# The first chunk of a convolution and mixture-of-experts kernel: another way of preparing it

## The reference, cut to what matters

```
conv: y = conv3x3(sign(ln_c(x)), sign(w) * sw)      # binarised, sw a power of two per channel
      mean, var = y over images and places, per channel
      clip((y - mean) * rsqrt(var + 1e-5) * gamma + beta, -1, 1)
ffn on tokens t (one per image and place, 64 channels), after a layernorm over channels:
      feat = mean over the 32 images               # per place
      w    = softmax(feat @ Wr + br)               # 8 experts, per place
      y    = for each expert: relu(bn(.@W1)) -> relu(bn(.@W2)) -> @Wo + bo
      sum over the experts with weights w
```

## Time and profile before

| what | us |
|---|---|
| median of 3 runs | 1387.19 (1386.34 to 1387.43) |
| the profiled execution, its own time | 1392.51 |
| its span, first to last instruction | 1390.7 |
| last convolution result copied by ACT, start | 168.69 |
| `t` of chunk 0, start | 178.27 |
| first `layer2` of chunk 0, start on PE | 218.24 |
| mean granted clock of TensorE, share of full | 0.982 |

### The profile page before, as it was taken

The page is one execution under the profiler, slowest core; times in us unless marked ns, Lnnn a source line. Parts: engine busy times, 40 slices in busy tenths (PEclk is TensorE's granted clock), DMA queues, the critical chain, the costliest instruction groups (busy, mean ns, idle before and its releaser), DMA issues. The chain is left out here.

```text
span 1390.7 us, 36592 instructions
## 1 busy us (share of the span) xinstructions
PE 1315.8 (95%) x14782; PEld 662.3 (48%) x14782; DVE 889.0 (64%) x1592; ACT 868.4 (62%) x1151; POOL 550.1 (40%) x474
## 2 busy tenths in 40 slices
PE   5899838999999999999999999999999999999997
PEld 3577613444544454445444444444454445444443
DVE  4344525676776666776667666666777666766665
ACT  4567645666666666666666666666666666666643
POOL 0514022344443444443444443444442544443441
PEclk9999958999999999999999999999999999999999
DMA  8978612232333232333232333232333223333121
GB/s 181 178 183 182 125 27 61 48 68 63 74 73 80 50 67 64 79 68 81 48 68 62 75 74 81 48 67 65 76 71 78 51 63 65 75 75 72 32 54 28
DMA packets 251009, 107.15 MB, mean 77 GB/s; under 512 B 238864, under 2 KB 239088, under 8 KB 250864
## 3 DMA queue, kind: packets, MB, share of 16 engines
q1 hardware_dynamic: 249600, 103.49, 35.4%
q0 software_dynamic: 1264, 1.61, 0.7%
HBM read 78.97 MB, written 26.09 MB: 76 GB/s over the span
## 5 line engine op out<-in xcount | busy, mean ns | idle before, releaser
L913 DVE SCALAR_TENSOR_TENSOR v<-ps,negb,wb 128x448 f32<-128x448 f32 x896 | 571.0, 678 | 298.7 <-PE ps L572 297.6
L743 ACT ACTIVATE h<-ps,bias 128x896 f32<-128x896 f32 x448 | 451.3, 1007 | 323.4 <-PE ps L550 323.4
L550 PE MATMUL ps<-xc,w 64*64 64x448 f32 x3584 | 463.0, 542 | 12.7 <-POOL xc L422 11.5
L588 PE MATMUL ps<-v,wo 64*64 64x448 f32 x3584 | 461.2, 540 | 3.9 <-issue 3.1
L572 PE MATMUL ps<-h,w 64*64 64x448 f32 x3584 | 457.3, 541 | 4.2 <-issue 1.8
L588 PEld LDWEIGHTS ps<-v,wo 64*64 64x64 f32 x3584 | 173.0, 133 | 186.5 <-issue 171.3
L550 PEld LDWEIGHTS ps<-xc,w 64*64 64x64 f32 x3584 | 163.6, 132 | 185.3 <-issue 179.9
L572 PEld LDWEIGHTS ps<-h,w 64*64 64x64 f32 x3584 | 169.4, 133 | 158.4 <-issue 141.1
L452 POOL TENSOR_TENSOR o<-o,upper 128x448 f32<-128x448 f32 x112 | 127.4, 1138 | 289.1 <-DVE o L923 289.1
L444 POOL TENSOR_TENSOR o<-xin,gconst 128x448 f32<-128x448 f32 x112 | 130.6, 1186 | 238.0 <-ACT gconst L786 144.2
L422 POOL TENSOR_TENSOR xc<-xc,spread 128x896 f32<-128x896 f32 x56 | 122.5, 2205 | 209.4 <-DMA spread<-rs_rows 209.4
(11 more groups left out here) (143 smaller groups left out, 669.0 us busy)
## 6 DMA issues: line engine op xcount, KB each, us to landing
xa<-in_x SPq DMA_DIRECT2D x64, 392.0 KB, 6.9
xin<-in_x SPq DMA_DIRECT2D x112, 224.0 KB, 4.1
spread<-rs_rows SPq DMA_DIRECT2D x112, 224.0 KB, 4.2
out<-o SPq DMA_DIRECT2D x224, 112.0 KB, 2.5
rs_rows<-rs SPq DMA_DIRECT2D x112, 3.5 KB
rows<-in_L_ffn_g POOLq DMA_DIRECT2D x2, 256.0 KB, 10.1
rows<-in_L_ffn_v POOLq DMA_DIRECT2D x2, 256.0 KB, 11.5
cwt<-in_L_conv_weight SPq DMA_DIRECT2D x2, 144.0 KB, 2.6
```

The lines of the kernel that those rows point to most:

```text
L550: last = mm(ps[64 * two:64 * two + 64, L1_BANKS + ab, 0:NG], w1[half, P * q + C * two:P * q + C * two + C], xc[half, s, g // 2, ab ^ (g % ...
L588: last = mm(ps[64 * par:64 * par + 64, ACC_BANKS + low, 0:NG], wo[rows_, 2 * Q + d, :], v[rows_, u % 2, par ^ (g % 2), d, :], start=(Q == ...
L743: A(h[:, u % 2, i], ps[:, L1_BANKS:L1_BANKS + 2, 0:NG], ACT.Relu, bias=bias[:, 0, q:q + 1]).then_inc(h_done[i], 1)
L913: last = V.scalar_tensor_tensor(out=v[:, u % 2, ab, d, :].rearrange("p (b w) -> p b w", w=W), in0=ps[:, L2_BANKS[ab] + d, 0:NG].rearrange( ...
```

## The change

Only what leads from the last convolved image to the body of chunk 0 is written anew; the loop over chunks is left, apart from the counts of three waits.

1. **Statistics in two portions.** DVE aggregates the first 28 images (`old_stats`, placed after the statistics of turn 13 of 0 to 15) while PE convolves the last four. After the last piece it aggregates only those four. The two are combined with weights 7/8 and 1/8: `MEANS` goes through `halves`, the two second moments through `halves_old` and `halves_new` into one sum in PSUM. Products of `SW`, `gamma`, `beta` that need no statistics are taken early, so two DVE instructions stand behind the reciprocal instead of six.
2. **Own banks.** The centrings of chunk 0 write banks 4, 5 and 0, 1 (`FIRST_BANKS`), without a wait between them.
3. **Square from PSUM by ACT, copy by DVE.** ACT squares PSUM straight into `spread`; DVE copies PSUM to `xc` after it.
4. **Deviations spread by TensorE.** `first_deviations`: 8 matmuls with the selection matrix `pick` copy the rows of `rs` over 64 partitions each into banks 2 to 5. The way over DRAM is gone for chunk 0.
5. **Products and features by DVE.** DVE multiplies `xc` by PSUM and sums the features; POOL and SP have no part in chunk 0's preparation.
6. **Order.** Logits come right after `layer1` of unit 0, ahead of chunk 1's centrings; chunk 1's `x1`, `centre` and `power` are put between the steps of chunk 0's gate.
7. Three small DVE instructions at the start of the kernel make `halves_old`, `halves_new` and `pick`.

The diff, cut to its core:

```diff
+        halves_old = sb("halves_old", [P, P], F32)
+        halves_new = sb("halves_new", [P, P], F32)
+        pick = sb("pick", [P, STEPS, 2, C], F32)
...
-        L1_BANKS, L2_BANKS, ACC_BANKS = 0, (2, 4), 6
+        L1_BANKS, L2_BANKS, ACC_BANKS, FIRST_BANKS = 0, (2, 4), 6, (4, 0)
+        LATE = 2
+        NEW_SHARE = LATE / TWOS
...
-            t=(0, 0, 0, 0), x1=(0, 0, 0, 0), centre=(1, 2), power=(1, 2),
-            var=3, root=3, square=3, inv=(3, 3), logits=5, gate=5, turn=5, wb=5)
+            t=(0, 0, 0, 0), x1=(0, 0, 0, 0), centre=(), power=(),
+            var=3, root=3, square=3, inv=(3, 3), logits=5, gate=6, turn=7, wb=8)
...
-                spread_rs(0, 0)
...
-                for p in range(STEPS):
-                    norm(0, 0, p)
-                feature(0, 0)
...
+                pe.wait_ge(a_stats, TWOS + 1)
+                mm(ps[:, 0, 0:1], halves[:], MEANS, start=True, stop=True).then_inc(s_pe, 1)
+                pe.wait_ge(a_stats, TWOS + 2)
+                mm(ps[:, 0, 1:2], halves_old[:], SQUARES[:, 0:1], start=True, stop=False)
+                mm(ps[:, 0, 1:2], halves_new[:], SQUARES[:, 1:2], start=False, stop=True).then_inc(s_pe, 1)
...
+                def first_centre(p):
+                    pe.wait_ge(x1_done, 2 * p + 2 + G)
+                    for low, high in TILES:
+                        rows_ = slice(64 * low, 64 * low + 64)
+                        g = 2 * p + (low ^ high)
+                        last = mm(ps[64 * high:64 * high + 64, FIRST_BANKS[p] + low, 0:NG], centre64[rows_, :],
+                                  xin[rows_, 0, BG * g:BG * g + BG, :], start=True, stop=True)
+                    last.then_inc(centre_done, 1)
+
+                def first_deviations():
+                    pe.wait_ge(rs_done, 1)
+                    pe.wait_ge(xc_kept, 1)
+                    for xy in range(2):
+                        for p, high in TILES:
+                            rows_ = slice(64 * p, 64 * p + 64)
+                            last = mm(ps[64 * high:64 * high + 64, L2_BANKS[xy] + p, 0:NG], pick[rows_, xy, high, :], rs[rows_, :],
+                                      start=True, stop=True)
+                    last.then_inc(first_spread, 1)
+
+                for p in range(STEPS):
+                    first_centre(p)
+                prep(AHEAD, 0, 0, AHEAD.var)
+                first_deviations()
...
-                prep_early(prep, 0, HALVES)
+                prep(AHEAD, 0, 0, AHEAD.logits)
+                prep(STEADY, 1, 1, STEADY.centre[0])
+                prep(AHEAD, 0, 0, AHEAD.turn)
                 pe.wait_ge(f_dve, 1)
-                prep(AHEAD, 0, 0, AHEAD.logits)
+                prep(AHEAD, 0, 0, AHEAD.wb)
+                prep(STEADY, 1, 1, STEADY.centre[1])
...
+                    A(spread[:, p], ps[:, bank:bank + 2, 0:NG], ACT.Square).then_inc(xc_done, 1)
...
+                def old_stats():
+                    dve.wait_ge(a_stats, TWOS - LATE)
+                    step(V.bn_aggr(OLD, stats[:, 0:2 * (TWOS - LATE)].rearrange("p b g s -> p (b g s)")))
+                    step(V.tensor_scalar(OLD_MEAN, OLD[:, 0:1], 1.0 - NEW_SHARE, None, ALU.mult))
+                    dve.wait_ge(s_ffn, 16 * N_FFN)
+                    step(V.tensor_scalar(SW2, SW, SW, None, ALU.mult))
...
+                step(V.bn_aggr(NEW, stats[:, 2 * (TWOS - LATE):].rearrange("p b g s -> p (b g s)")))
...
+                step(V.tensor_scalar(SCALE, bn[:, 15:16], SWG, None, ALU.mult))
+                V.scalar_tensor_tensor(out=OFFSET1, in0=MINUS_MEAN, scalar=SCALE, in1=BETA1, op0=ALU.mult, op1=ALU.add).then_inc(s_bn, 1)
...
+                    V.tensor_copy(xc[:, 0, p], ps[:, bank:bank + 2, 0:NG]).then_inc(xc_kept, 1)
...
+                    V.tensor_tensor(xc[:, 0, p], xc[:, 0, p], ps[:, Y + p:Z + p + 1:Z - Y, 0:NG], ALU.mult).then_inc(u_done[p], 1)
...
+                step(V.tensor_tensor(feat2[:], xc[:, 0, 0], xc[:, 0, 1], ALU.add))
+                for half in (NG // 2, NG // 4):
+                    step(V.tensor_tensor(feat2[:, :, 0:half], feat2[:, :, 0:half], feat2[:, :, half:2 * half], ALU.add))
+                V.tensor_tensor(feat[:], feat2[:, :, 0:W], feat2[:, :, W:2 * W], ALU.add).then_inc(feat_done, 1)
```

More of the change, by code:

```diff
@@ L237, in prep_point @@
                 prep(STEADY, k + 2, s, half)
-        def prep_ahead(prep):
-            for h in range(AHEAD.logits):
-                prep(AHEAD, 0, 0, h)
-        def prep_early(prep, first, end):
-            for h in range(first, end):
-                prep(STEADY, 1, 1, h)
         with nc.Block() as block:
@@ L878, in _ @@
                 dve.wait_ge(s_pe, 2)
[L879 to L884 removed]
+                step(V.tensor_copy(MEAN, ps[:, 0, 0:1]))
@@ L885, in _ @@
+                step(V.tensor_scalar(DEVS, bn[:, 18:22:2], MEAN, None, ALU.subtract))
+                for n, part in enumerate((OLD, NEW)):
+                    last = V.scalar_tensor_tensor(out=SQUARES[:, n:n + 1], in0=DEVS[:, n:n + 1], scalar=DEVS[:, n:n + 1], in1=part[:, 1:2],
+                                                  op0=ALU.mult, op1=ALU.add)
+                last.then_inc(a_stats, 1)
+                step(V.tensor_scalar(MINUS_MEAN, MEAN, -1.0, None, ALU.mult))
                 dve.wait_ge(s_pe, 3)
-                V.tensor_scalar(bn[:, 13:14], ps[:, 0, 1:2], SW, None, ALU.mult).then_inc(d_bn, 1)
@@ L893, in _ @@
[L893 to L900 removed]
+                step(V.reciprocal(bn[:, 15:16], bn[:, 11:12]))
```

99 lines of the change are left out of this document (56 added, 43 removed).

## The result

The changed kernel takes 1381.78 us (median of 15 runs, 1378.53 to 1386.52), the kernel before beside it 1387.9 us (15 runs, 1384.59 to 1396.47). The ratio is 0.9948, interval 0.9934 to 0.9963, that is 7.2 us less (5.1 to 9.2) where 11.0 were forecast: faster, as said, but above the range. The profiled execution took 1384.15 us, with a span of 1382.4, against 1392.51 and 1390.7: 8.3 less.

The account below looks back on a forecast made before the run. PE bounds the body; a serial 55.6 us passage before it was to shrink. Gains 2.5 + 2.3 + 4.5 + 4.35, less 1.1 and 1.6, make 11.0 us off the 1387.19 us median: 1376.2 us, range 1373.9 to 1379.2.

Parts of the forecast that it names:

- 1 statistics to `t`: Statistics chain to the start of `t`: aggregating 96 values instead of 768, less added small steps, gains 2.5 us.
- 2 to the variance matmul: From `t` through chunk 0's centrings to the variance matmul: 6.5 us instead of 8.84, gaining 2.3 us.
- 3 `rs` to the first `h`: From `rs` to the first hidden layer's result: 6.45 us without DRAM instead of 10.96, gaining 4.5 us.
- first to second `h`: Second half of `layer1` follows the first by 2.94 us as before, so no change.
- 4 second `h` to the logits: Logits follow `layer1`'s second result by 0.27 us instead of 4.62, gaining 4.35 us.
- 5 logits to `wb`: Chunk 1's first centring goes between logits and `wb`: 6.85 us instead of 5.74, giving back 1.1 us.
- 6 `wb` to the second `h` of the loop: Chunk 1's second centring delays the loop's second `h`: 6.0 us behind `wb` instead of 4.38, giving back 1.6 us.
- rival of the earlier clock: Deviations' second half, `layer1` and one centring at full clock: 1.5 to 2 us more gained, 1374.4 us; chance 0.18.
- second statistics matmul: In the statistics chain, a second matmul with another 128x128 weight was put at 0.3 us of added cost.
- VectorE's products: Rival: chunk 0's products take 2.05 us each, features late, aggregation and average 0.5 us more: 1379.2 us; chance 0.14.
- held at the table switch: Rival: `t` follows the table load only after another 1.28 us; gain 9.7 us, time 1377.5 us; chance 0.03.
- Slower: Rival: shifted phase between PE, POOL and transfers costs 0.55 us at each of 27 chunk handovers: 1391 us; chance 0.02.

Follow-up runs that it names:

- number 7: wide version with 16 empty semaphore increments on TensorE ahead of the statistics matmul, against the wide version without them: 1381.43 us, ratio 0.9931 to the kernel before.
- number 4: Changed kernel with 220 empty semaphore increments at the start of TensorE's stream: 1397.31 us, ratio 1.0063; estimated some 1376 without the start delay.
- wide version: Changed kernel with deviations spread by 4 matmuls of 128 weight columns instead of 8 of 64, 16 TensorE instructions less: 1371.60 us, ratio 0.9866.
- number 12: Changed kernel and wide version, each without the result stores of chunks 0 to 26: 1370.68 and 1366.14 us, one run each.

## Why the prediction was right and where it failed

The working of the passage held step by step (us, forecast / measured):

| step | forecast | measured |
|---|---|---|
| 1 statistics to `t` | -2.5 | -2.64 |
| 2 to the variance matmul | -2.3 | -2.41 |
| 3 `rs` to the first `h` | -4.5 | -4.65 |
| first to second `h` | 0 | -0.79 |
| 4 second `h` to the logits | -4.35 | -4.45 |
| 5 logits to `wb` | +1.1 | +0.38 |
| 6 `wb` to the second `h` of the loop | +1.6 | +1.28 |

The two estimates that had no row of their own were near: the aggregation of 96 values took 0.59 us (0.5), the product with PSUM over 896 columns 1.04 (1.1). Two terms came out better by 0.8 and 0.7 us, and both from the clock: the second half of `layer1` and a centring of chunk 1 run at full clock (0.98 us for groups that took 1.77 at half clock); the first half does from 193.8 us on. That was the rival of the earlier clock, which I put at 1.5 to 2 us, with a chance of 0.18; it came, and its size was right. The argument against it, that a block of 3.3 us gave the full clock only when it was over, did not carry over: here PE had worked 5.5 us without a break when it came (188.3 to 193.8), and the block was not over. The 0.3 us for the second statistics matmul had no row either; it started 0.45 us behind the first. VectorE's products were not dear. Nor was ScalarE held at the table switch: 174.98 + 1.28 = 176.26, and `t` starts at 176.27. The 1.38 us of the Trainium skill (ScalarE: Activation LUTs, What ACT_TABLE_LOAD costs) are not to be seen here, even with the DVE steps gone that might have hidden them.

The step that failed is the sentence on which the sum was carried to the end: "Whatever shortens the chain of that passage moves the whole body forward by as much. Nothing in the body is tied to a clock of its own". The chain of the passage is 13.3 us shorter and the end comes 8.3 earlier. What the body is tied to is the place of its code in the blocks that TensorE fetches: from the second `h` of the loop to the end it took 1173.7 us, where it was to stay as before, 1169.4. The prediction's rival *Slower* had the right symptom, dearer handovers from chunk to chunk (6.3 us over the 27, or 0.23 each, where 0.4 each decides), the wrong cause (a phase between engines), and a dismissal that the runs refute: "body instructions and their order are the same". They are, in both kernels of number 7, and the one takes 9.8 us more. With the body at the old place the number would have come out, some 1376 us by number 4, but not for the reasons given: behind the last `y` copy that kernel is 17.2 to 18.7 us shorter than the kernel before, not 11.0, of which the passage has 13 to 14 and the loop 4 to 5, and with a convolution that ends at 165.9 us, as it does in some executions, the same estimate gives some 1372. That it meets 1376.2 is luck.

The handovers show the place as cause, by repeats, by a shift of 36 in the old kernel, of 256 in it, and of 16 in the wide one. That most of the cost needs the stores is shown by number 12, one execution each (6.2 of 9.8 us); that a block then comes late is the likely way and not shown. Open are the rest, why equal places still differ by up to 3.7 us in the handovers and by up to 5 us from the second `h` to the end, and why the changed kernel's handovers are 2 to 3 us cheaper than the old one's at places 0 and 132, but 1.4 to 1.6 dearer at 36.

## What to carry to other kernels

In a long unrolled program an edit ahead of the body also moves the body's code, and here that was worth 5.7 us in the old kernel (36 instructions) and 9.8 in the wide one (16), where the edit was worth 13 in its own stretch: price the edit in the stretch that it touches, time the stretch behind it apart, and measure each version at two or three code places (some increments of an unused semaphore, put where the engine waits anyway) before crediting or blaming it. Look for instruction fetches on the page; where they run through the whole span, a cheap change of the number of instructions is a thing to tune by itself, as the wide version shows (1371.60 us against 1382.40, at an equal passage). In a serial passage, a spread by the idle TensorE into PSUM, where the product reads it, beat the way over DRAM by 3.35 us of 9.66, even at half clock.

## What the runs showed of the hardware

- TensorE's code came in 105 blocks of 16 KB (the changed kernel), in the loop over chunks one every 11.8 us. In the 27 handovers PE stopped 23 times for 0.15 to 1.14 us with no releaser, 20 times of these 1 to 3 us behind the start of a fetch.
- By where the blocks' borders fell among its instructions, an unchanged loop took 1125.5 or 1135.2 us for its 27 handovers (wide version, 16 instructions apart), and in the old kernel 1128.0 to 1129.0 or 1133.7 (36 apart).
- An increment of a semaphore on TensorE at the kernel's start costs about 0.1 us (220 of them 21 us) once the wait there is filled (36 of them cost nothing, the convolution ended at 165.91 us); 96 of them in three waits of the passage cost nothing that shows (passage 40.21, the changed kernel's two 39.36 and 40.18).
- Sixteen matmuls with 64x64 weights take 3.27 us and eight with 64x128 weights 3.36, at half clock and with 448 columns each: two with 64x64 weights took the time of one with 64x128.
- VectorE's product over 896 columns took 1.04 us with an operand in PSUM and 1.09 with both in SBUF; POOL's took 2.05 each in the kernel before.
